# Identity matmuls in TensorE's queue, one PSUM bank instead of two in three cores, and new tables of order, in a 14-layer kernel

## What is computed

```python
x = x + 0.5 * L0_ffn(norm(x))    # top-k of 1024 patterns, twice, one output row per batch
x = x + L0_attn(norm(x))         # blocks of 32 queries and 64 keys, relative embedding
x = x + 0.5 * L0_ffn(norm(x))
x = x + 0.5 * L1_ffn(norm(x))    # causal attention, then top 2 of 8 experts
x = x + L1_attn(norm(x))         # causal linear attention: scores * tril, no softmax
x = x + 0.5 * L1_ffn(norm(x))
x = x + 0.5 * L2_ffn(norm(x))    # top 1 of 8 experts, hidden 512
x = x + L2_attn(norm(x))         # attention in blocks of 32
x = x + 0.5 * L2_ffn(norm(x))
x = x + 0.5 * L3_ffn(norm(x))    # two layers of windowed attention and a gated MLP
x = x + L3_attn(norm(x))         # full attention
x = x + 0.5 * L3_ffn(norm(x))
```

## Time and profile before

| | us |
|---|---|
| median of 3 runs | 3175.35 (3172.24 to 3183.04) |
| the profiled execution | 3180.55 |
| its span, first to last instruction | 3178.7 |
| TensorE busy | 2708.7 (85%) |
| VectorE busy | 2222.8 (70%) |
| ScalarE busy | 1704.1 (54%) |
| GpSimd busy | 799.8 (25%) |
| mean granted TensorE clock | 0.897 |

### The profile page before, as it was taken

How to read it: one execution, slowest core, us unless ns; L and a number is a source line. 1 busy time by engine, 2 the same in 40 slices (tenths; PEclk the granted TensorE clock), 3 DMA queues, 4 the chain that set the end, 5 groups by cost and what they waited for, 6 DMA issues and landing times.

```text
span 3178.7 us, 64037 instructions
## 1 busy us (share of the span) xinstructions
PE 2708.7 (85%) x24501; PEld 1719.0 (54%) x24561; DVE 2222.8 (70%) x5316; ACT 1704.1 (54%) x4158; POOL 799.8 (25%) x809
## 2 busy tenths in 40 slices
PE   5867788899987789998877888899998888999996
PEld 2645455544444544467855787566663332556664
DVE  4656567778876667765566446888787777788883
ACT  2235443565622366643357434677775566776772
POOL 1010001111111211101222114655441112555540
PEclk8767787899986799998899989999998888999997
DMA  2523310000000000036700466010100000101010
GB/s 106 221 38 69 67 48 1 1 1 1 1 1 1 1 1 1 10 111 238 245 19 1 152 229 204 18 26 16 26 16 2 1 1 1 24 16 26 17 33 11
DMA packets 134794, 159.36 MB, mean 50 GB/s; under 512 B 82901, under 2 KB 109781, under 8 KB 132954
## 3 DMA queue, kind: packets, MB, share of 16 engines
q1 hardware_dynamic: 131962, 150.08, 15.5%
q0 software_dynamic: 2048, 4.20, 0.4%
q10 hardware_dynamic: 480, 0.98, 0.1%
HBM read 106.53 MB, written 30.61 MB: 43 GB/s over the span
## 4 chain that ended last, share of the span: by engine, by line
PE 49%; DVE 22%; ACT 10%; issue 6%; POOL 4%; DMA 3%; SPq 0%; DVEq 0%; POOLq 0%; ACTq 0%; another core or an unknown queue 0%
DVE nm L1190 5%; PE ps L1149 4%; PE ps L534 3%; PE ps L1922 3%; PE ps L2124 3%; PE ps L1126 3%; ACT hand L498 3%; PE ps L1090 3%; PE ps L2290 3%; PE ps L387 2%; PE ps L611 2%; PE ps L266 2%; DVE pre L2210 2%; PE ps L1520 2%; PE ps L2427 2%
## 5 line engine op out<-in xcount | busy, mean ns | idle before, releaser
L1190 DVE TENSOR_REDUCE nm<-ps 128x2 f32<-128x256 f32 (+2 forms) x704 | 424.8, 636 | 97.8 <-PE ps L1090 54.7
L1239 ACT ACTIVATE core<-ps 128x512 f32<-128x512 f32 x672 | 359.3, 589 | 91.4 <-PE ps L1131 55.8
L328 POOL TENSOR_TENSOR rstd<-ve,weights 128x4 f32<-128x4 f32 x80 | 81.1, 1014 | 941.5 <-DVE ve L305 921.7
L2196 POOL TENSOR_TENSOR pre<-pre,sin 128x512 f32<-128x512 f32 x128 | 238.1, 1881 | 258.3 <-ACT pre L2167 218.1
L1090 PE MATMUL ps<-hand 128*128 128x128 bf16 (+4 forms) x989 | 236.7, 316 | 42.0 <-DVE nm L1190 37.7
L498 ACT COPY hand<-ps 64x512 bf16<-64x512 bf16 x336 | 194.9, 580 | 135.4 <-PE ps L534 86.9
L1126 PE MATMUL ps<-hand 128*128 128x128 bf16 (+4 forms) x999 | 214.1, 304 | 11.6 <-ACT hand L498 6.3
L2330 ACT ACTIVATE core<-ps,nm 128x128 f32<-128x128 f32 x512 | 182.2, 377 | 68.3 <-DVE nm L2347 67.8
L2201 POOL TENSOR_TENSOR ss<-ss,weights 128x16 f32<-128x16 f32 x64 | 196.4, 3068 | 71.0 <-DVE ss L2216 69.1
L2124 PE MATMUL ps<-weights,pre 128*128 128x512 f32 x384 | 205.1, 637 | 5.8 <-ACT pre L2170 3.4
L1149 PE MATMUL ps<-core,hand 128*32 128x512 f32 (+3 forms) x2048 | 181.7, 450 | 8.1 <-ACT otok L1222 4.1
(11 more groups left out here) (346 smaller groups left out, 6695.8 us busy)
## 6 DMA issues: line engine op xcount, KB each, us to landing
hand<-in_experts SPq DMA_DIRECT2D x72, 836.0 KB, 4.9
shear<-post SPq DMA_DIRECT2D x64, 256.0 KB
core<-in_experts SPq DMA_DIRECT2D x16, 836.0 KB, 7.4
core<-shear SPq DMA_DIRECT2D x128, 64.0 KB, 2.3
hand<-hand SPq DMA_DIRECT2D x16, 512.0 KB, 4.4
hand<-hand SPq DMA_DIRECT2D x16, 384.0 KB, 5.6
pre<-sorted_in SPq DMA_DIRECT2D x8, 704.0 KB, 6.1
sorted_out<-core SPq DMA_DIRECT2D x88, 64.0 KB
```

The costliest lines, as they stand in the source:

```text
L1190: nc.vector.tensor_reduce(nm_of(unit), src, AX.X, ALU.max, negate=True).then_inc(negmax, 1)
L1239: nc.scalar.activation(prob8[:, i % PROBS, 0:w], m.ps[:, RING[at % NR], 0:w], ACT.Exp).then_inc(ring_out, 1)
L2196: ins = nc.gpsimd.tensor_tensor(o[:, :, :, z:z + hl], x[:, :, :, y0:y0 + hl], sn[:, t, :, z:z + hl].unsqueeze(2).to_broadcast([P, 2, LH, h ...
```

## The change

1. **Fillers.** A new stream at the end of a slot's list issues matmuls on TensorE whose weights are the bf16 identity and whose moving operand is the identity twice, 256 columns, into columns 256 to 511 of a bank that the slot does not use. Nothing reads them, and they have no wait but the stream's `after`, which is the core of the slot before (for the last core's slot the pre).

```diff
+FILL = 256
+FILL_AT = {"l0_ffn": 4, "l0_attn": 3, "l1_attn": 5, "l2_ffn": 5}
+def fillers(nc, m, bank, n):
+    out = m.ps[:, bank, L - FILL:L].rearrange("p (a b) -> p a b", b=P)
+    def tensor(pe):
+        for _ in range(n):
+            yield 0.0
+            nc.tensor.matmul(out, m.identb, m.identb.unsqueeze(1).to_broadcast([P, FILL // P, P]), start=True, stop=True)
+    return [(1.0, dict(tensor=tensor))]
...
+            streams = [(after, parts) for after, parts in streams if parts]
+            bank = FILL_AT.get(names[units[k][0]]) if 0 <= k < len(units) else 2
+            if k == len(units) - 1:
+                bank = 6
+            if bank is not None and k != 1:
+                order = ORDERS[SLOT_ORDERS[k]].get("tensor", "") if k in SLOT_ORDERS else ""
+                n = sum(c for i, c in runs(order) if i == len(streams))
+                streams.append((before.pre if k == len(units) - 1 else before.core, fillers(nc, m, bank, n)))
+            return streams
```

2. **Single banks**, which leave a bank for the fillers:

```diff
-    S, PT, O = (0, 1), (2, 3), (4, 5)
+    S, PT, O = (0, 1), 2, (4, 5)
...
-            if u >= 2:
-                pe.wait_ge(pT_ready, u - 1)
+            if u >= 1:
+                pe.wait_ge(pT_ready, u)
...
-                out = m.ps[:, 4 + g % 2, t * P:(t + 1) * P]
+                out = m.ps[:, 4, t * P:(t + 1) * P]
+                if i == 1:
+                    pe.wait_ge(state_ready, NT - 1)
...
-                if t == 0 and g >= 2:
-                    pe.wait_ge(o_out, g - 1)
+                if t == 0 and g >= 1:
+                    pe.wait_ge(o_out, g)
...
-            if i >= 2:
-                pe.wait_ge(out_ready, i - 1)
+            if i >= 1:
+                pe.wait_ge(out_ready, i)
...
-                ins = nc.tensor.matmul(m.ps[:, 4 + i % 2, 0:D], acts[:, i % 2, c, :], w2(i, c), start=(c == 0),
+                ins = nc.tensor.matmul(m.ps[:, 4, 0:D], acts[:, i % 2, c, :], w2(i, c), start=(c == 0),
```

3. **Orders.** Slots -1, 0, 1, 2 and 56 get tables; 38 of the 53 slots 3 to 55 get another string on TensorE, VectorE, ScalarE or GpSimd, with or without fillers (7 to 10, 15, 26 to 30, 38, 39 and 43 to 45 keep theirs), and SyncE's are written out in more slots. Three of them, TensorE's of slot 17 and of slot 56, ScalarE's of slot 17:

```diff
-    "tensor": "c1a1c1b1a1b1a2b1a1b1a1b1a2c2b1a1b1a1b1a1b1a1b1a1b1a1b1a1b1a1b1a2",
+    "tensor": "e6a1c1b1e1a1e3b1e4a2b1c1b1e2b1a2c1e1a1e25a1e1a1e2c1e3a1e8a1e2a1e15b1e1a1b1a1b1e1a1e1b1e5b1a1b1e5b1"
+               "a1b1e5b1a1e8",
...
-     "scalar": "b8a1b2a1b4a2",
+     "scalar": "b6a1b1a1b3a1b4a1",
...
+    {"tensor": "a4b64a1b3a2b7a1b4a1b8a1b6a1b7a1",
```

More of the change, by code:

```diff
@@ L188, in program, with started, in_order @@
         begun += span
-def in_order(name, eng, streams, order):
+def started(name, eng, streams):
     steps = [program(stream, name, eng) for stream in streams]
-    for s in steps:
-        next(s, None)
+    for step in steps:
+        next(step, None)
+    return steps
+def in_order(name, eng, streams, order, begun=None, following=None, gate=None):
+    steps, ahead = begun or started(name, eng, streams), None
     for i, n in runs(order):
+        if i < 0 and ahead is None:
+            gate(eng)
+            ahead = started(name, eng, following)
         for _ in range(n):
-            next(steps[i], None)
+            next(steps[i] if i >= 0 else ahead[i + AHEAD], None)
+    return ahead
+AHEAD = ord("a") - ord("A")
 def runs(order):
@@ L1453, in scalar @@
                     act.wait_ge(av, u - NTS + 1)
-                nc.scalar.copy(pT[:, u % NTS, :], bank(m, PT[u % 2])).then_inc(pT_ready, 1)
+                nc.scalar.copy(pT[:, u % NTS, :], bank(m, PT)).then_inc(pT_ready, 1)
             if i >= WEIGH and (i - WEIGH) < U and units[i - WEIGH][1] == 1:
@@ L1733, in scalar @@
                 before.read(act)
-            nc.scalar.copy(a.otok[:, g, :], bank(m, 4 + g % 2)).then_inc(o_out, 1)
+            nc.scalar.copy(a.otok[:, g, :], bank(m, 4)).then_inc(o_out, 1)
     def done(eng):
@@ L2525 @@
[L2525 to L2536, removed]
@@ L2552 @@
[L2552 to L2563, removed]
@@ L2731 @@
+    {"tensor": "a2b4a4b1d8b1a1b1a1b1d2a1d3b1d12b1d3b1d8b1d2a1d5a1d8",
+     "vector": "a2b1a1b1a1b4a1b1a4b5a2",
+     "scalar": "a5b1a1b1a1b1a1b2a2",
+     "gpsimd": "b1c1",
+     "sync": "b2"},
+    {"tensor": "a4b64a1b3a2b7a1b4a1b8a1b6a1b7a1",
+     "vector": "a12",
+     "scalar": "a5",
+     "gpsimd": "a1",
+     "sync": "a2"},
 ]
@@ L3120, in streams_of @@
                 streams.append((nothing, [(1.0, dict(gpsimd=keep))]))
-            return [(after, parts) for after, parts in streams if parts]
+            streams = [(after, parts) for after, parts in streams if parts]
[7 more added lines that the diff above has]
+            return streams
         for k in range(-1, first):
@@ L3127, in macaron @@
         sets = [[nc.alloc_semaphore(f"set{i}_{n}") for n in range(SET)] for i in range(3)]
-        cleared = ctx.enter_context(nc.semaphore("cleared"))
+        cleared, opened = (ctx.enter_context(nc.semaphore(n)) for n in ("cleared", "opened"))
         passed = {e: ctx.enter_context(nc.semaphore(f"passed_{e}")) for e in ("tensor", "vector", "scalar", "gpsimd", "sync")}
@@ L3136, in all_slots, with gate @@
         def all_slots(name, eng):
+            ahead = None
             for k, streams in slots:
-                merge(name, eng, streams, ORDERS[SLOT_ORDERS[k]] if k in SLOT_ORDERS else {})
-                if first + 2 <= k < len(units):
-                    eng.wait_ge(cleared, k - first - 1)
+                def gate(eng, early=True):
+                    if first + 2 <= k < len(units):
+                        eng.wait_ge(cleared, k - first - 1)
+                        if early:
+                            eng.sem_inc(opened, 1)
+                ahead = merge(name, eng, streams, ORDERS[SLOT_ORDERS[k]] if k in SLOT_ORDERS else {}, ahead,
+                              slots[k - first + 1][1] if k < len(units) else None, gate)
+                if ahead is None:
+                    gate(eng, False)
                 eng.sem_inc(passed[name], 1)
```

379 lines of the change are left out of this document (220 added, 159 removed), and 7 rows, old and new, of the table SLOT_ORDERS.

## The result

The changed kernel takes 3137.52 us (median of 3, 3133.79 to 3139.21) against 3175.35: 0.9874 of it, 95% interval [0.9851, 0.9898]. That is 37.8 us less where I had forecast 47. The profiled execution spans 3135.7 us.

A forecast was written before the change was run, and what follows sets the result against it. TensorE, 49% of the chain and at its lower clock for a fifth of the time, bounds the kernel; -64 + 12 + 10 - 5 = -47 gives 3128 us on the scale of the medians, range 3070 to 3180.

The forecast's parts named there:

- Where the low time is, and that fillers remove it: In 13 stretches of slots with fillers, 343 us at the lower clock, of which three quarters would go.
- The last slot: Its 36 us of low clock cost 9 us; its L2427 matmuls would take near 640 ns instead of 1141.
- The fillers' net worth: In the 15 slots with fillers, 64 us less from the clock and 12 us more for their cost.
- the rate of 0.25: In slots that get fillers, each us of low clock removed shortens the time by 0.25 us; ends 0.2 and 0.32.
- half a filler per run: At 293 runs the next real matmul starts late by this on average: 16 us, 8 on the chain.
- Slots 16 and 25, where they don't fit: 12.9 us of filler into 8.9 idle and 14.5 into 6.2; a third of the 12 us counted.
- Single banks: Waits for one bank in three cores: l0_attn 4 us, l1_attn 5, l2_ffn 1; 10 us more, ends 0 and 60.
- Orders: New tables in slots -1 to 2 give 5 us less; other slots nothing, with 20 us kept to both sides.
- rival 1: In the filler slots the clock rises but the path moves to VectorE and ScalarE: 3166 us, chance 0.15.
- Rival 2: In stretches that stay at 1.2 GHz the fillers, 216 ns each, become the delay: 3215 us, chance 0.10.
- Rival 3: In l1_attn ScalarE's copy comes late for a single bank, 40 us instead of 5: 3172 us, chance 0.08.

The follow-up runs named there:

- double_columns: The changed kernel with fillers of 512 columns in place of 256, same number and places; 1.0215 of the kernel before.
- trimmed: The changed kernel with 931 fillers in place of 1605, those cut that ended after the next real matmul's last wait; 0.9911 of the kernel before.
- half_columns: The changed kernel with fillers of 128 columns in place of 256, same number and places; 0.9963 of the kernel before.
- head_tables: The kernel before with only the changed kernel's tables for slots -1 to 2, without fillers; 0.9968 of the kernel before.
- no_fill: The changed kernel without its 1605 fillers, its single banks and orders kept; 0.9981 of the kernel before.
- no_fill_two_banks: The changed kernel without fillers and with two banks again in all three cores, only its orders left; 0.9947 of the kernel before, 3162.86 us.
- fewer_slots: The changed kernel without the fillers of slots 3, 5, 6 and 25 (628 of 1605); 0.9895 of the kernel before.
- two_banks_elsewhere: The changed kernel with two banks again in slot 7 and the expert cores of slots 27 and 35; 0.9852 of the kernel before.
- combined: The changed kernel with two banks in slots 7, 27, 35, five old tables, and shorter filler runs in slots -1, 6, 34; 0.9806 of the kernel before, 3114.59 us.

## Why the prediction was right, and where it was not

The runs split the change into -33 us for fillers, +11 for single banks and -17 for orders, in sum -39; the forecast had -52, +10 and -5, in sum -47. The direction and the mechanism, fillers that bring TensorE's clock back, were right. That the total came out so near is luck: two misses of opposite sign partly cancel, 19 us too much for the fillers and 12 too little for the orders.

- *Where the low time is, and that fillers remove it:* right. I took three quarters; 269 of 339 us went, 0.79 (0.76 by the second profile, with 82 us left). Slots 4, 5, 6, 16, 17 and 19 are above 0.9; slot 18 is not, it has 0.80. The mean reached 0.947, not 0.96.
- *The last slot:* right. 9 us forecast, 8.8 and 11.3 in two traces; its 128 x 512 products take 645 ns where I had said 640:

```profile
L2460 PE MATMUL ps<-post,weights 128*128 128x512 f32 x8 | 4.5, 645 | 1.7 <-ACT post L2475 1.1 <-ACT post L376 0.6
```

- *The fillers' net worth:* the step that failed. I had 64 less 12; it is 33. With the rate of 0.25 the 269 us are worth 67, and the price would be 34, the very end of my range; by the trace's 25.5 it would be 42. That the price is mis-sized is supported by `double_columns` and by the chain, which gives L263 58 us, 2% of the span (the 81 us of the expectations also counted fillers that run beside a real matmul of the chain), and 10% in `double_columns`. In slot 3 alone, the chain by line:

```profile
by line: PE ps L263 24.0%; PE ps L915 18.5%; PE ps L565 6.5%; PE ps L418 5.5%; PE ps L935 4.2%; PE ps L1320 3.8%; PE ps L1006 3.8%; DVE pre L469 3.3%; DVE pre L477 3.3%; DVE hand L529 3.1%; ACT hand L529 2.2%; DVE core L809 1.9%; DVE hand L
```

  A quarter of that slot's path is fillers, in part those at its end. I had set their 173 us against 199 us of idle time as if both were one sum, and charged half a filler per run; but idle time lies where it lies, and when the matmuls before it get faster, data are ready sooner and the same run of fillers ends later than they are. By the trace of the changed kernel, with the count that `trimmed` was made from, real matmuls start 109 us later in sum than their waits would let them, behind fillers that are busy for 230.

  The rate of 0.25 is in doubt too. At that rate the low time that came back in `half_columns`, from 70 to 179 us, is worth 27 us, all of the 28 by which it was slower, and halving every filler would have given back nothing. Slot 47 has the same queues and no filler in the kernel before and in `head_tables`:

```profile
2641.90:2729.10 87.20, 77.57 (x381) 24.77 (x381) 65.80 (x113) 56.07 (x107) 34.13 (x33) 0.88 0.05 11
```
```profile
2625.30:2707.50 82.20, 72.86 (x384) 23.57 (x387) 65.60 (x113) 56.07 (x107) 34.11 (x33) 0.96 0.05 12
```

  TensorE's idle time is 9.6 and 9.3 us, the low time 20.9 and 6.6, and the slot is 5.0 us shorter: 0.35 per us. Slot 18, in the two profiles of the last section, gives 0.38. At 0.36 the 269 us would be worth 97 and the price would be 64; this is an estimate, since no kernel here raises the clock of the filler slots without fillers, and how the 33 us divide into gain and price stays open between 67 less 34 and 97 less 64. In either case the price is some three to five times the 12 that I had.
- *Slots 16 and 25, where they don't fit:* slot 25 is 4.4 us longer by TensorE's queue, as much as its last 41 fillers take (41 x 0.108), and slot 26 is 7.3 us shorter; slot 16 stayed within 0.4. The rows of slot 25 alone don't show that my rule held.
- *Single banks:* right in size, 10 against 11, with an error of some 9. The place was not: I had given l0_attn 4 us over four slots, and slot 7 alone loses 5 to 8, to ScalarE's lateness of the earlier trace rows, which I had named and left to the upper end. Its strings were not recut, unlike those of slots 4 to 6, for which `no_fill` and `no_fill_two_banks` differ by 0.8 us at most.
- *Orders:* -5 against -17 [-23, -11]. For the head I had read the right rows, 39.5 against 35.2 and 33.0 us, which make 4.3 to 6.5 for one slot, and then taken 5 for all of them because of the barrier and of the DMA share of 0.57. That discount was wrong: slots 1 and 2 gained 6.1 each with more DMA in the same stretch, 0.67. The recut strings of the others are worth 7 us, inside the 20 that I kept.
- *Rivals.* VectorE's share of the chain rose from 22% to 25%, but in `no_fill` it is 25% too, so that shift is not from the clock; rival 1 is not what took the gain. Rival 2 did not come: two neighbouring fillers are 109 ns apart, and the clock held. What cost part of the gain is fillers that delay real matmuls although the clock is high, as their 109 us of lateness say. Here the measurement decides against the rule of the Trainium skill, "TensorE: Matmul & The Clock Gate", section "A second HAM failure mode: psum-queue depth-cycling", as a forecast for this kernel: groups of matmuls with short gaps between them, 2 to 9 us of idle time in a slot, kept 0.94 to 1.00 in slots 3 to 6. Rival 3's late copy did come, in l0_attn and not in l1_attn.

## What to carry to other kernels

Matmuls that nobody reads can hold TensorE's clock, but their worth is the difference of two terms of one size, here between 67 less 34 and 97 less 64 us; size each run for the gap as it will be at the faster clock, read the end of a stretch from more than one engine when its last work is fillers, and test the amount on both sides, since half and double the columns were both worse. Give up a double buffer only where the freed bank is used: slot 7 had one bank and no filler, and paid some 6 us for nothing. And when one kind of work stands in the trace with and without a tuned order, believe that pair of rows before any reason to discount it.

## What the runs showed that I had not expected

The clock of a stretch depends on how the one before it ended. Slot 4 has 0.97 and 51.0 us behind slot 3 with its fillers, 0.90 and 58.0 us behind slot 3 without them, its own queue of instructions being the same (3.1 of these 7.0 us are the moved end of slot 3). The low time stands at its start; these are its first 15.1 us in `fewer_slots` and in the changed kernel:

```profile
197.20:212.30 15.10, 11.22 (x71) 8.07 (x72) 5.76 (x18) 1.64 (x7) 2.14 (x4) 0.61 0.60 100
```
```profile
199.20:214.30 15.10, 14.53 (x198) 10.98 (x196) 8.84 (x17) 7.86 (x21) 3.15 (x6) 1.00 0.53 99
```

Also, the same queues can run in two ways. Slot 18 of the changed kernel took 50.6 us at a clock of 0.80; the same instructions in the same slot took 44.3 at 0.96 in `two_banks_elsewhere`, where nothing was changed between slots 7 and 27, and 50.6 again in `combined`. What decides between them is not shown. In `two_banks_elsewhere`:

```profile
969.00:1013.30 44.30, 38.06 (x409) 24.05 (x408) 30.68 (x63) 12.70 (x27) 6.62 (x7) 0.96 0.01 2
```

So one profile tells a slot's length within some 6 us only, and a gain of 5 us read from one slot of one profile has to come back in others before it is believed.
